# Two-layer graph network on one core: sort ends at groups of 1024 edges, rests of q by TensorE, node update and gated sum rearranged

## The chip, the core and the metric

The kernel runs on one core of a Trainium2 chip. A core has TensorE (PE, matmuls into PSUM; its weight loads have a row of their own, PEld), VectorE (DVE), ScalarE (ACT), GpSimd (POOL) and SyncE (SP, which issues DMAs); each runs its own list of instructions and waits on semaphores for the others. 16 DMA engines move data between the off-chip memory and the on-chip one (SBUF). The metric is the device time of one execution in microseconds (us), the median of several.

## The reference, cut to what matters

A graph attention layer over 200,000 edges that come sorted by `dst`, then a second layer: a small attention over 131,072 unsorted edges, whose sums choose 2 of 4 experts per node.

```python
# layer 1 (6250 nodes, 256 channels, 8 heads), x normalised first
q, k, v = x @ Wq + bq, x @ Wk + bk, x @ Wv + bv
logits = einsum('ehd,ehd->eh', q[dst], k[src]) / sqrt(32)
attn = segment_softmax(logits, dst)
agg = segment_sum(attn * v[src], dst)
h = gelu(agg + x @ Wskip + bskip);  y = x + h;  x2 = layernorm(y) * gamma + beta   (+ the layer's input)
# layer 2, on layernorm(x2)
h = x2n @ W_gat;  a_src, a_dst = sums of h * att_src, h * att_dst
e = leaky_relu(a_src[src] + a_dst[dst]);  alpha = segment_softmax(e, dst)
scores = mean over heads of layernorm(segment_sum(h[src] * alpha, dst) + b_gat)
gates = softmax of the 2 largest of 4 scores, 0 for the others
out = x2 + sum over the 4 experts of gates[e] * (gelu(x2n @ W1[e] + b1[e]) @ W2[e] + b2[e])
```

## The kernel before, in words

Five stages run one after the other, each a block at whose end all engines meet. Nodes are padded to 49 windows (`NW`) of 128 rows, and 7 windows (`CW`) form one of 7 blocks (`NB`).

**prepare** (L201 to L529) does three things at once. (1) For each of 49 windows ("tiles") it normalises x (ACT L542), turns it on TensorE (L474), and makes k and v in one PSUM bank and q and skip in another (L498 the bias, L500 the fp32 products). ACT evacuates both banks (`evacuate`, L562 to L567). q is kept as three bf16 parts whose sum is q: the high part is a cast by ACT (L562), POOL subtracts it (L271), ACT casts that rest into the middle part (L552), and POOL makes the low part with a second subtraction (L275). (2) DVE sorts the 131,072 edges of layer 2 by a bitonic network over a [128, 1024] array of keys `dst << 13 | src`. A step is a minimum and a maximum (L307, L308; L311, L312 where the direction turns). Steps across partitions need the array turned; a `flip` is 8 transposes on TensorE (L514) which DVE (L354) and ACT (L611) copy back, half each. There are 15 flips (`FLIPS`). TensorE does tiles and flips in one fixed order: the table `BETWEEN` says how many tiles stand ahead of each flip, and DVE waits where TensorE comes late. (3) Small tables for the walks over edges, made through `tab_ps`.

**attend** walks over groups of 512 edges of layer 1; POOL gathers their k and v rows. Its loop is the same before and after.

**node_update** (L1097 to L1285) makes x2 and its normalised, transposed form block by block. SP loads `xs` (x, skip and the layer's input, 2688 KB a block, L1107) behind five loads of constants (L1100 to L1104). DVE divides the sums by their denominators, adds skip (L1180), ACT applies gelu, and DVE and ACT normalise twice. At a block's end ACT normalises into `xn2` (L1224), TensorE transposes 14 squares of it (L1278), ACT copies them out (L1231), and TensorE multiplies by `wg` (L1285); each of these waits for the whole of the one ahead.

**route_experts** (L1384 to L1618): POOL gathers one row of a 20-column table per edge of layer 2, 128 edges an instruction, 1024 instructions (L1396). Groups of 8 columns (`RG`, 1024 edges) are summed into windows by one-hot matmuls, a step for each pair of group and window, and the experts' matmuls run between. Ahead of its first gather POOL takes a maximum over the partitions (`partition_all_reduce`, L1386), for which it waits for DVE (L1503).

**route_gates** (L1675 to L1776) makes the gates on DVE, then out = x2 + the four gated expert rows: 28 DVE instructions a block (7 windows, 4 experts, L1776) over four buffers (`SLOTS`); the first buffer is filled at the end of route_experts. SP loads blocks 1 to 3, and then in one list stores block i (L1691), waits for that store to land, and loads block i + 4 (L1683, L1684). It first loads three small rows `rg_con` (L1679).

## Time and profile before

| what | us |
|---|---|
| median of 3 runs | 3990.57 (3986.79 to 3992.12) |
| the profiled execution | 3987.74, of which the span 3985.9 |
| stage prepare | 0 to about 341 |
| attend | about 341 to 2390 |
| node_update | 2390 to 2560 |
| route_experts | 2560 to 3873 |
| route_gates | 3873 to 3986 |

The profile is one execution. A view of stretches gives for each engine its busy time and its instructions in brackets, the TensorE clock granted (1.00 is full speed) and what the DMA engines moved. A timeline gives start, duration, engine, line and operation; the bracket at a row's end is the idle time of the engine ahead of it and what ended it. A row of a line says how often it ran, its busy time and its mean in ns.

### The profile page before, as it was taken

The page shows a single profiled execution, that of the slowest core. Times are in us where ns is not written, and L with a number is a line of the kernel's source. Part 1 is how long each engine was busy: PE and PEld are TensorE (multiplying, and loading weights), DVE is VectorE, ACT ScalarE, POOL GpSimd, SP SyncE. Part 2 cuts the span into 40 slices and gives each one's busy share as a digit, 9 for nine tenths or more (in the row PEclk, how much of TensorE's full clock was granted, in tenths as well). Part 3 has the DMA queues.
Part 4 walks back from the last instruction along what each step waited for, and adds up shares of the span by engine and source line. Part 5 has one row for each costly group of instructions (what it writes and reads, how often), then busy time and mean ns, then how long its engine had stood idle before and what let it go on. Part 6 is the DMA issues. An engine that isn't in the chain of part 4 may idle for free. (4 is left out here: it accounts for less than half of the span.)

```text
span 3985.9 us, 106539 instructions
## 1 busy us (share of the span) xinstructions
PE 3324.8 (83%) x26108; PEld 2449.2 (61%) x26109; DVE 3352.4 (84%) x8812; ACT 2563.2 (64%) x6745; POOL 2589.5 (65%) x2730
## 2 busy tenths in 40 slices
PE   7886999999999999999999992488888888887620
PEld 2334888888788888878888872455555555554410
DVE  8886999999999999999999998667766667666448
ACT  5435888888788888878888875455555555554310
POOL 3225777777677777777777742277777777777750
PEclk9898999999999999999999995599999999999855
DMA  6536888888888888888888857211111111111148
GB/s 218 191 130 200 255 260 256 259 256 261 242 257 255 262 257 257 253 246 257 257 258 258 259 175 246 70 23 33 32 33 32 29 33 33 33 28 33 23 94 309
DMA packets 367692, 683.52 MB, mean 171 GB/s; under 512 B 70294, under 2 KB 240482, under 8 KB 367074
## 3 DMA queue, kind: packets, MB, share of 16 engines
q0 software_dynamic: 157888, 427.05, 38.9%
q1 hardware_dynamic: 183106, 223.68, 16.6%
q10 hardware_dynamic: 26080, 25.70, 2.2%
q8 instruction: 247, 4.05, 0.4%
q14 instruction: 371, 3.04, 0.2%
HBM read 588.41 MB, written 87.78 MB: 170 GB/s over the span
## 5 line engine op out<-in xcount | busy, mean ns | idle before, releaser
L746 POOL DMA_INDIRECT KV<-kv_d,src_i x1564 | 1478.9, 946 | 536.0 <-issue 472.9
L1396 POOL DMA_INDIRECT re_src<-src_tab_d,rsrc x1024 | 982.4, 959 | 312.0 <-issue 244.3
L1012 PE MATMUL agg_ps<-msg,oh 128*128 128x264 f32 x3512 | 889.9, 396 | 1.7 <-DVE agg_ps L830 1.7
L1012 PEld LDWEIGHTS agg_ps<-msg,oh 128*128 128x128 f32 x3512 | 631.6, 190 | 87.5 <-ACT oh L921 1.9
L965 PE MATMUL Q<-q,ohT 128*128 128x256 bf16 x5328 | 659.0, 274 | 1.7
L907 ACT ACTIVATE square<-iota_b,off 128x128 bf16<-128x128 bf16 x1784 | 569.3, 392 | 0.3
L847 DVE TENSOR_REDUCE lg<-prod 128x32 f32<-128x1024 f32 x443 | 540.5, 1220 | 15.3
L835 DVE TENSOR_TENSOR msg<-KV,weigh_ps 128x1056 f32<-128x1056 f32 x439 | 542.5, 1236 | 8.0 <-issue 7.8
L843 DVE TENSOR_TENSOR prod<-KV,Q 128x1024 f32<-128x1024 f32 x443 | 532.6, 1202 | 17.6 <-POOLq L737 13.2
L965 PEld LDWEIGHTS Q<-q,ohT 128*128 128x128 bf16 x5328 | 492.1, 98 | 61.0 <-issue 0.5
L1618 PE MATMUL ex_y_ps<-ex_w,ex_hid 128*112 128x256 f32 x1792 | 440.7, 389 | 0.0
L1606 PE MATMUL ex_h<-acc,ex_w 128*128 (+1 forms) x896 | 417.5, 592 | 3.3 <-PEq L1097 3.3
L1535 ACT COPY re_ohT<-re_ohT_ps 128x1024 bf16<-128x1024 bf16 x179 | 181.1, 1012 | 351.8 <-PE re_ohT_ps L1580 351.1
L891 ACT COPY acc<-agg_ps 128x264 f32 x439 | 166.1, 378 | 329.3 <-PE agg_ps L1012 322.8
L1618 PEld LDWEIGHTS ex_y_ps<-ex_w,ex_hid 128*112 128x112 f32 x1792 | 302.3, 179 | 53.7
L910 ACT ACTIVATE oh<-square,one 128x512 bf16<-128x512 bf16 x446 | 322.0, 722 | 14.5
L921 ACT CAST oh<-oh 128x512 f32<-128x512 bf16 x439 | 273.0, 622 | 0.0
L1434 DVE TENSOR_SCALAR re_oh<-iota_b,re_off 128x128 bf16<-128x128 bf16 x1432 | 254.6, 276 | 6.4
L1580 PE MATMUL re_ohT_ps<-ident_b,re_oh 128*128 128x128 bf16 x1432 | 121.2, 233 | 163.3 <-DVE re_oh L1434 158.0
L914 ACT COPY ohT<-ohT_ps 128x512 bf16<-128x512 bf16 x445 | 255.3, 574 | 3.2 <-PE ohT_ps L955 3.2
L1580 PEld LDWEIGHTS re_ohT_ps<-ident_b,re_oh 128*128 128x128 bf16 x1432 | 89.4, 104 | 232.7 <-DVE re_oh L1434 203.7
L1606 PEld LDWEIGHTS ex_h<-acc,ex_w 128*128 128x128 f32 x896 | 163.0, 202 | 97.1 <-issue 96.6
(264 smaller groups left out, 5662.8 us busy)
## 6 DMA issues: line engine op xcount, KB each, us to landing
q<-q_d SPq DMA_DIRECT2D x446, 192.0 KB
y_d<-ex_y ACTq DMA_DIRECT2D x56, 448.0 KB
KV<-kv_d,src_i POOLq DMA_INDIRECT x1564
nu_xs<-xs_d SPq DMA_DIRECT2D x7, 2688.0 KB, 11.6
rg_ye<-y_d SPq DMA_DIRECT2D x5, 3584.0 KB, 15.6
re_src<-src_tab_d,rsrc POOLq DMA_INDIRECT x1024
kv_d<-pr_kv SPq DMA_DIRECT2D x49, 260.0 KB, 2.2
xs_d<-pr_xs SPq DMA_DIRECT2D x49, 256.0 KB, 2.3
```

Of the source, the lines that this page charges most:

```text
L746: pool.indirect_dma_start(out=KV[:, t % (KVR * G), :], out_offset=None, in_=k.kv_d, in_offset=bass.IndirectOffsetOnAxis(ap=k.src_i[:, t:t ...
L835: v.tensor_tensor(m[:, :, :, :], KV[:, tiles(s), D:KVW].rearrange("p t (h e) -> p t h e", e=HW), bc(p_ps.rearrange("p (t h) -> p t h", h=H ...
L843: v.tensor_tensor(prod[:, :, :], KV[:, tiles(s), 0:D], Q[ring(s, 2)][:, :, :], ALU.mult).then_inc(ok["prod"], 1)
L847: v.reduce_sum(lg[s.slot][:, :], prod[:, :, :].rearrange("p t (h d) -> p (t h) d", d=DH), AX.X).then_inc(ok["lg"], 1)
L907: q = act.activation(square[:, t, :], k.iota_b[:, :], ACT.Square, bias=off[s.slot][:, t:t + 1])
L910: act.activation(oh[ring(s, OHR)][:, :, :], square[:, :, :], ACT.Relu, bias=k.one[:, :], scale=-1.0).then_inc(ok["oh"], 1)
L921: act.copy(oh32[ring(s, 2)][:, :, :], oh[ring(s, OHR)][:, :, :]).then_inc(ok["oh32"], 1)
L965: m = pe.matmul(Q[ring(s, 2)][:, t, :], ohT[ring(s, OHR)][:, t, :], q3[s.slot][:, c * D:(c + 1) * D], start=(c == 0), stop=(c == 2))
L1012: m = pe.matmul(agg_ps[:, 0:HEADS * HW], oh32[ring(s, 2)][:, t, :], msg[ring(s, 2)][:, t, :, :].rearrange("p h e -> p (h e)"), start=False ...
L1396: pool.indirect_dma_start(out=gs[:, t % (RING * RG), :], out_offset=None, in_=k.src_tab_d, in_offset=bass.IndirectOffsetOnAxis(ap=k.rsrc[: ...
L1606: m = pe.matmul(h_ps[f % 2][:, 0:UN], k.w1_sb[:, u.at % NE, c, f * P:(f + 1) * P], k.xT[:, bass.ds(u.block, 1), c, half * UN:(half + 1) * ...
L1618: m = pe.matmul(y_ps[w % 2][0:YN, 0:D], hid[u.at % 2][:, f, w * YN:(w + 1) * YN], k.w2_sb[:, u.at % NE, f, :], start=(f == 0), stop=(f == ...
```

## The change

1. **Sort.** Level 17 of the sort ends once each group of 1024 edges holds its own range of keys: the last ten steps and the last two flips are gone (`FLIPS` 13), and the walk's tables take the group's largest dst (a maximum over 8 columns, a transpose, a maximum, a matmul) and not its last one. The edges of a group lie in another order.
2. **q's rests.** TensorE subtracts the high part and then the middle part from q in its PSUM bank, as a product with minus the identity (`less_hi`, `less_mid`), and ACT casts both rests (`middle`, `lowest`). POOL has no tile work left; ACT has no copy `qf`. The skip part is evacuated second and no longer last. `BETWEEN` has new numbers, and three tiles stand behind the last flip.
3. **node_update.** The first load is cut into three columns of 896 KB and goes ahead of the constants; the first division stands ahead of the wait for the constants; the work at a block's end (normalise, transpose, copy, multiply) is in two parts of 4 and 3 windows.
4. **route_experts.** The maximum over partitions is a transpose, a DVE maximum and a matmul; POOL's gathers wait for nothing of it. SP loads the three small rows here.
5. **route_gates.** Of 7 windows DVE sums 6 (`VT`), TensorE the seventh with diagonal matrices of gates, which ACT makes and whose sum ACT copies out. ACT issues the stores on its own queue, SP only waits for them and loads.

On TensorE in prepare, one tile in the middle of its first twenty; `pr_qs_ps` holds q and skip, `pr_xt` the turned x. Before:

```order
L474 MATMUL pr_xt_ps<-ident,pr_xs0 128x128 x2
L498 MATMUL pr_kv_ps1<-pr_b_parts,pr_ones3 128x512
L500 MATMUL pr_kv_ps1<-pr_w,pr_xt1 128x512 x2
L498 MATMUL pr_qs_ps1<-pr_b_parts,pr_ones3 128x512
L500 MATMUL pr_qs_ps1<-pr_w,pr_xt1 128x512 x2
```

After, with the other window's bank named beside it:

```order
L468 MATMUL pr_xt_ps<-ident,pr_xs4 128x128 x2
L481 MATMUL pr_kv_ps1<-pr_b_parts,pr_ones3 128x512
L483 MATMUL pr_kv_ps1<-pr_w,pr_xt1 128x512 x2
L489 MATMUL pr_qs_ps0<-pr_q3_0,minus_b 128x256
L481 MATMUL pr_qs_ps1<-pr_b_parts,pr_ones3 128x512
L483 MATMUL pr_qs_ps1<-pr_w,pr_xt1 128x512 x2
L493 MATMUL pr_qs_ps0<-pr_q3_0,minus_b 128x256
```

Two bf16 products of 256 columns have come into each tile, both for the window ahead: one between the two banks, one behind them.

On DVE, the end of the sort; the last exchange that is in both, and what follows. Before:

```order
L308 TENSOR_TENSOR so_key<-so_key 128x512
L307 TENSOR_TENSOR so_key<-so_key 128x2x256
L308 TENSOR_TENSOR so_key<-so_key 128x2x256
L307 TENSOR_TENSOR so_key<-so_key 128x4x128
L308 TENSOR_TENSOR so_key<-so_key 128x4x128
L354 COPY so_key<-so_flip 128x512
L307 TENSOR_TENSOR so_key<-so_key 128x8x64
L308 TENSOR_TENSOR so_key<-so_key 128x8x64
```

After:

```order
L298 TENSOR_TENSOR so_key<-so_key 128x512
L425 TENSOR_SCALAR so_dst_i<-so_key 128x1024
L427 CAST rdst<-so_dst_i 128x1024
L429 TENSOR_REDUCE so_most<-rdst 128x128
L431 TENSOR_SCALAR rsrc<-so_key 128x1024
L433 TENSOR_REDUCE so_event<-pp_tab 128x1
```

Three steps, a flip, seven steps and a flip have gone, and two maxima have come in.

On SP in route_gates, from the first store on. Before:

```order
L1691 DMA out_dram<-acc 128x7x256
L1683 DMA acc<-y_d 128x7x1024
L1684 DMA acc<-x_d 128x7x256
L1691 DMA out_dram<-rg_o 128x7x256
L1683 DMA rg_ye<-y_d 128x7x1024
L1684 DMA rg_o<-x_d 128x7x256
L1691 DMA out_dram<-rg_o 128x7x256
```

After, from the load of block 4 on:

```order
L1734 DMA acc<-y_d 128x7x1024
L1735 DMA acc<-x_d 128x7x256
L1734 DMA rg_ye<-y_d 128x7x1024
L1735 DMA rg_o<-x_d 128x7x256
L1734 DMA rg_ye<-y_d 128x7x1024
L1735 DMA rg_o<-x_d 128x7x256
```

The stores have left SP's list and stand in ACT's, each behind the copy of its block's seventh window.

The core of the diff:

```diff
-        FLIPS = 15
+        FLIPS = 13
-        BETWEEN = (20, 2, 2, 2, 2, 2, 2, 2, 2, 2, 2, 2, 2, 2, 3)
+        BETWEEN = (20, 2, 2, 2, 2, 2, 2, 2, 2, 3, 2, 3, 2)
...
-                for w in range(NW + 1):
-                    if w < NW:
-                        pool.wait_ge(ok["qf"], w + 1)
...
-                        pool.tensor_tensor(resid[w % 2][:, :], qf[w % 2][:, :], q3[w % PS][:, 0:D], ALU.subtract).then_inc(ok["resid"], 1)
...
-                        pool.tensor_tensor(q3[u % PS][:, 2 * D:3 * D], resid[u % 2][:, :], q3[u % PS][:, D:2 * D], ALU.subtract).then_inc(ok["lo"], 1)
...
+                    if level < 17:
+                        for b in (9, 8, 7):
+                            plain(P << (b - 7))
+                        flip(meanwhile.get(held["flips"], lambda: None))
+                        for b in range(6, -1, -1):
+                            plain(1 << b)
...
+                def less_hi(w):
+                    pe.wait_ge(ok["hi"], w + 1)
+                    pe.wait_ge(ok["skip"], w + 1)
+                    pe.matmul(qs_ps[w % 2][:, 0:D], k.minus_b[:, :], q3[w % PS][:, 0:D], start=False, stop=True, skip_group_check=True).then_inc(ok["less_hi"], 1)
+
+                def less_mid(w):
+                    pe.wait_ge(ok["mid"], w + 1)
+                    pe.matmul(qs_ps[w % 2][:, 0:D], k.minus_b[:, :], q3[w % PS][:, D:2 * D], start=False, stop=True, skip_group_check=True).then_inc(ok["less_mid"], 1)
...
+                    project(kv_ps[p], p, 0)
+                    if w:
+                        less_hi(w - 1)
+                    if w >= 2:
                         pe.wait_ge(ok["skip"], w - 1)
+                        pe.wait_ge(ok["lo"], w - 1)
+                    project(qs_ps[p], p, 2 * D).then_inc(ok["products"], 1)
+                    if w:
+                        less_mid(w - 1)
...
+                for at, sem in ((D, skip_in), (0, landed[0]), (2 * D, landed[0])):
+                    sp.dma_start(xs[0][:, :, at:at + D], k.xs_d[0:CN, at:at + D].rearrange("(w p) f -> p w f", p=P)).then_inc(sem, 16)
                 sp.dma_start(gam[:, :], bc(gamma.unsqueeze(0), [P, D])).then_inc(const, 16)
...
+                quotients(0, 0)
+                v.wait_ge(const, 80)
...
-                pe.wait_ge(xt_ok, i + 1)
...
+                    for w in range(CW):
+                        if w in (0, parts[1][0]):
+                            pe.wait_ge(xt_ok, i * 2 + (1 if w == 0 else 2))
...
-                pool.wait_ge(ok["max_in"], 1)
-                pool.partition_all_reduce(peak[:, 1, :], peak[:, 0, :], P, bass.bass_isa.ReduceOp.max).then_inc(ok["max"], 1)
...
+                for i in range(SLOTS, NB):
+                    sp.wait_ge(stored[i % SLOTS], (i // SLOTS) * 16)
+                    load(i)
...
+                for i in range(NB):
+                    act.wait_ge(summed, i + 1)
+                    act.copy(o[i % SLOTS][:, VT, :], sum_ps[i % 2][:, 0:D]).then_inc(a_ok, 1)
+                    if i + 2 < NB:
+                        factors(i + 2)
+                    store(i)
...
+                    pe.matmul(sum_ps[i % 2][:, 0:D], k.ident[:, :], o[s][:, VT, :], start=True, stop=False)
+                    for e in range(NE):
+                        m = pe.matmul(sum_ps[i % 2][:, 0:D], diag[i % 2][:, e, :], ye[s][:, VT, e, :], start=False, stop=(e == NE - 1))
```

## Rows read from the trace of the kernel before

**Rows 1.** Four stages: length, busy time of PE, PEld, DVE, ACT, POOL, clock, DMA

```profile
0.00:343.00 343.00, 273.46 (x761) 117.28 (x762) 288.45 (x497) 149.66 (x462) 99.69 (x127) 0.93 0.50 172
...
2390.00:2560.30 170.30, 63.94 (x294) 60.37 (x295) 127.36 (x334) 95.92 (x162) 29.17 (x15) 0.54 0.55 184
2560.30:3873.00 1312.70, 1004.12 (x6952) 645.75 (x6952) 848.50 (x3792) 642.84 (x803) 982.95 (x1026) 0.93 0.19 31
3873.00:3985.90 112.90, 0.00 (x0) 0.00 (x0) 96.53 (x227) 4.13 (x5) 0.00 (x0) 0.50 0.86 313
```

**Rows 2.** Timeline of prepare, DVE: end of the sort, and attend's first instruction

```profile
310.47 0.69 DVE L307 TENSOR_TENSOR so_key<-so_key 128x512 f32<-128x512 f32 x1
...
332.04 1.07 DVE L354 COPY so_key<-so_flip 128x512 f32<-128x512 f32 x1 [3.91 <-PE so_flip L514]
333.58 0.69 DVE L438 TENSOR_SCALAR so_dst_i<-so_key 128x1024 int32<-128x1024 int32 x1 [0.47 <-ACT so_key L611]
...
341.11 0.28 DVE L871 MEMSET msg<- 128x264 f32 x1 [0.41 <-PEq L198]
```

**Rows 3.** Groups of prepare: count, busy us, mean ns; then line 308 alone, min/median/max

```profile
L308 DVE TENSOR_TENSOR so_key<-so_key 128x512 f32<-128x512 f32 x136 | 108.1, 795 | 0.0
...
L308 DVE TENSOR_TENSOR so_key<-so_key x136: 677/684/1194, 47.8 to 327.4; 128x512 f32<-128x512 f32 x136
```

**Rows 4.** Timeline of prepare, POOL and DVE over one tile

```profile
301.15 1.11 POOL L275 TENSOR_TENSOR pr_q<-pr_resid,pr_q 128x256 bf16<-128x256 f32 x1
...
301.66 1.15 DVE L308 TENSOR_TENSOR so_key<-so_key 128x512 f32<-128x512 f32 x1
```

**Rows 5.** Timeline of prepare, TensorE: one tile, the first flips, the last tile

```profile
45.50 0.38 PE L474 MATMUL pr_xt_ps<-ident,pr_xs 128*128 128x128 f32 x2
...
48.36 1.98 PE L500 MATMUL pr_qs_ps<-pr_w,pr_xt 128*128 128x512 f32 x4
50.18 0.38 PE L474 MATMUL pr_xt_ps<-ident,pr_xs 128*128 128x128 f32 x2
...
135.15 1.97 PE L514 MATMUL so_flip<-ident,so_key 128*128 128x128 f32 x8 [9.25 <-DVE so_key L308]
...
149.18 1.04 PE L514 MATMUL so_flip<-ident,so_key 128*128 128x128 f32 x8
...
329.58 1.98 PE L500 MATMUL pr_qs_ps<-pr_w,pr_xt 128*128 128x512 f32 x4
```

**Rows 6.** Timeline of attend, TensorE: twelve bf16 products of 256 columns

```profile
364.86 1.47 PE L965 MATMUL Q<-q,ohT 128*128 128x256 bf16 x12
```

**Rows 7.** Timeline of node_update: its first large load, the add that waits for it

```profile
2392.79 1.04 SPq L1107 DMA_DIRECT2D nu_xs<-xs_d  x2
...
2403.53 2.02 DVE L1180 TENSOR_TENSOR nu_out<-nu_out,nu_xs 128x1792 f32<-128x1792 f32 x1 [3.80 <-DMA nu_xs<-xs_d]
```

**Rows 8.** Timeline of node_update: the last block's end

```profile
2543.93 3.55 ACT L1224 ACTIVATE nu_xn<-nu_x,nu_shift,nu_rstd 128x256 f32<-128x256 f32 x7 [0.47 <-DVE nu_shift L1162]
...
2547.53 3.25 PE L1278 MATMUL nu_turn<-ident,nu_xn 128*128 128x128 f32 x14 [3.75 <-ACT nu_xn L1224]
...
2552.71 4.25 PE L1285 MATMUL nu_h<-nu_wg,acc 128*128 128x24 f32 x28 [1.93 <-ACT acc L1231]
```

**Rows 9.** Timeline of route_experts, POOL: the maximum; then line 1396 alone

```profile
2566.37 0.39 POOL L1386 PARTITION_ALL_REDUCE rt_top<-rt_top  x1 [5.94 <-issue]
...
L1396 POOL DMA_INDIRECT re_src<-src_tab_d,rsrc x1024: 940/944/1490, 2566.9 to 3860.2; - x171
```

**Rows 10.** Timeline of route_gates, DVE: waits, the first and the last block's sum

```profile
3881.24 0.97 DVE L1720 TENSOR_TENSOR rg_s<-rg_s,rg_con 128x784 f32<-128x784 f32 x1 [2.78 <-DMA rg_con<-in_L_ffn_ln_beta_dram]
...
3896.12 11.17 DVE L1776 SCALAR_TENSOR_TENSOR acc<-acc,gates 128x256 f32<-128x256 f32 x28
...
3967.57 11.17 DVE L1776 SCALAR_TENSOR_TENSOR rg_o<-rg_ye,gates,rg_o 128x256 f32<-128x256 f32 x28 [4.86 <-DMA rg_o<-x_d]
```

**Rows 11.** Stretches of route_gates, columns as in Rows 1

```profile
3905.00:3910.00 5.00, 0.00 (x0) 0.00 (x0) 5.00 (x14) 0.00 (x0) 0.00 (x0) 0.50 1.03 409
...
3915.00:3920.00 5.00, 0.00 (x0) 0.00 (x0) 5.00 (x14) 0.00 (x0) 0.00 (x0) 0.50 0.35 90
```

**Rows 12.** DMA issues: KB each, us to landing; of route_gates, then of 0 to 40 us

```profile
out_dram<-acc SPq DMA_DIRECT2D x2, 896.0 KB, 11.7
...
so_ends<-in_L_ffn_edge_index_dram SPq DMA_DIRECT2D x1, 1024.0 KB, 14.1
...
pr_b_parts<-pr_b_part ACTq DMA_DIRECT2D x3, 2.0 KB, 5.2
```

More of the change, by code:

```diff
@@ L158, in prepare @@
         xt = [sb(f"pr_xt{i}", [P, 2, P], F32) for i in range(2)]
-        qf = [sb(f"pr_qf{i}", [P, D], F32) for i in range(2)]
-        resid = [sb(f"pr_resid{i}", [P, D], F32) for i in range(2)]
         xt_ps = ps("pr_xt_ps", [P, 2, P], F32)
@@ L195, in order @@
                 flip(f)
-            assert w == NW
+            while w < NW:
+                tile(w)
+                w += 1
         with nc.Block() as block:
@@ L484, in rows, with project @@
                     t.then_inc(ok["turned_rows"], 1)
+                def project(bank, p, at):
+                    pe.matmul(bank[:, :], ones3[:, :], b_parts[:, at:at + 2 * D], start=True, stop=False)
+                    for c in range(2):
+                        m = pe.matmul(bank[:, :], xt[p][:, c, :], w_sb[:, c, at:at + 2 * D], start=False, stop=(c == 1))
+                    return m
+                def less_hi(w):
[5 more added lines that the diff above has]
+                    pe.matmul(qs_ps[w % 2][:, 0:D], k.minus_b[:, :], q3[w % PS][:, D:2 * D], start=False, stop=True, skip_group_check=True).then_inc(ok["less_mid"], 1)
                 def tile(w):
@@ L523, in _ @@
                 order(tile, flip)
+                less_hi(NW - 1)
+                less_mid(NW - 1)
                 pe.wait_ge(ok["table"], table_at["lasts"])
                 pe.wait_ge(ok["sort"], ready[FLIPS][0])
-                pe.matmul(tab_ps[:, 0:RNG], ends[:, :], k.rdst[:, RG - 1:RT:RG], start=True, stop=True).then_inc(ok["tab_products"], 1)
+                pe.transpose(tab_ps[:, 0:P], r_most[:, :], k.ident[:, :]).then_inc(ok["tab_products"], 1)
                 pe.wait_ge(ok["sort"], ready[FLIPS + 1][0])
+                pe.matmul(tab_ps[:, P:P + RNG], ones[:, :], r_most[:, :], start=True, stop=True).then_inc(ok["tab_products"], 1)
+                pe.wait_ge(ok["sort"], ready[FLIPS + 2][0])
                 pe.matmul(tab_ps[:, 0:RNS], ones[:, :], r_passed[:, :], start=True, stop=True).then_inc(ok["tab_products"], 1)
@@ L566, in evacuate @@
                              kv_ps[p][:, D:2 * D].rearrange("p (h d) -> p h d", d=DH)).then_inc(ok["kv"], 1)
-                    act.copy(xs[w % LOOP][:, D:2 * D], qs_ps[p][:, D:2 * D]).then_inc(ok["skip"], 1)
                 def rows(b):
@@ L1190, in turn @@
                     v.wait_ge(s_gelu, i + 1)
+                    if first and s == 0:
+                        v.wait_ge(landed[0], FIRST_ROWS)
                     ch.on(v.tensor_tensor(out[s][:, :, :], out[s][:, :, :], xs[s][:, :, 0:D], ALU.add))
@@ L1240, in turn @@
                     act.wait_ge(back, i * KB + SHIFT)
-                    normalise(0, out[s], x2[s]).then_inc(norm, 1)
+                    normalise(0, out[s], x2[s], 0, CW).then_inc(norm, 1)
                     if not (first and s == 0):
@@ L1247, in turn @@
                     act.wait_ge(back, (i + 1) * KB)
-                    normalise(1, x2[s], xn2).then_inc(xn_ok, 1)
+                    for a, b in parts:
+                        normalise(1, x2[s], xn2, a, b).then_inc(xn_ok, 1)
                 gelu(0, 0)
@@ L1641, in body @@
                         hidden(u.next(), 3)
+                pe.wait_ge(ok["max_in"], 1)
+                pe.transpose(d_ps[0][0:RH, 0:P], peak[:, :], k.ident[:, :]).then_inc(ok["max"], 1)
+                pe.wait_ge(ok["max_in"], 2)
+                pe.matmul(d_ps[1][:, 0:RH], ones[:, :], peak_diag[:, :], start=True, stop=True).then_inc(ok["max"], 1)
                 pe.wait_ge(k.weights, 64)
@@ L1651, in _, with route_gates @@
                 walk(pe, body)
-def route_gates(nc, k, b_gat, ln_gamma, ln_beta, out):
+def route_gates(nc, k, out):
     with ExitStack() as ctx:
@@ L1827, in graph_layers @@
         k.o0 = free[:, CW * NE * D:CW * (NE + 1) * D].rearrange("p (w f) -> p w f", f=D)
+        at = CW * (NE + 1) * D
+        k.diag = [free[:, at + i * NE * P:at + (i + 1) * NE * P].rearrange("p (e n) -> p e n", n=P) for i in range(2)]
         with ExitStack() as route:
@@ L1840, in graph_layers @@
                 route_experts(nc, k)
-            route_gates(nc, k, b_gat, ln_gamma, ln_beta, out)
+            route_gates(nc, k, out)
 _INS = ["x", "src", "dst"] + ["L0_gnn_" + n for n in ("Wq", "bq", "Wk", "bk", "Wv", "bv", "Wskip", "bskip", "gamma", "beta")] \
```

221 lines of the change are left out of this document (124 added, 97 removed).

## Prediction

> **What bounds the kernel now.** I read the stretches by stage first [rows 1]. The change leaves attend's loop alone, so the four stages shown there are what it can move: 341 us of prepare, 170 of node_update, 1313 of route_experts, 113 of route_gates. Each has another limit, and the average of the engines over the span says little.
>
> In **prepare** DVE (288 us of 343) and TensorE (273) are both near full [rows 1]. The timeline shows who waits for whom. TensorE stood 9.25 us ahead of the first flip, until DVE had sorted [rows 5]: DVE's sort is the bound there. At the last flip it is the other way, DVE waits 3.91 us for TensorE, which was making its last tiles [rows 2]. So the sort sets the end, with TensorE close behind. In **node_update** DVE is the busiest (127 of 170), and only the ends leave room: a wait of 3.80 us for the first load [rows 7], and at the last block a chain ACT, TensorE, ACT, TensorE with nothing beside it [rows 8]. In **route_experts** POOL issues 1024 gathers from 2566.9 to 3861.1, 1.264 us each, of which 0.944 are the instruction [rows 9]: it is the pace, and what delays its first gather delays the stage. In **route_gates** DVE sums for 11.17 us a block, seven times, behind about 23 us of gate arithmetic, with two waits, 2.78 and 4.86 us, for DMA [rows 10].
>
> **Part 1, the sort.** Ten steps and two flips go. They lie between the exchange at 310.47 and the one that reads the keys at 333.58 [rows 2]: 23.1 us of DVE's path. A maximum over 8 columns, one over a transpose and a product come in; the nearest rows are of 0.7 to 1.1 us for 1024 columns [rows 2] and less for the small ones, so about 2 us with their hand-overs.
>
> **Part 2, POOL out of the tiles.** An exchange of line 308 takes 0.684 us at the median and up to 1.194, with a mean of 0.795 [rows 3]; the slow ones are those that lie beside a POOL subtraction, as the one of 1.15 us beside 301.15 [rows 4]. Two readers of the same memory seem to hold each other up. 136 x (0.795 - 0.684) is 15 us for this line alone, and its twin, line 307, runs as often: some 30 us of DVE's path go with POOL's work. By parts 1 and 2 the sort could end near 341.1 - 23 - 30 + 2 = 290. It will not, since TensorE is now late.
>
> **Part 3, TensorE's own sum.** One tile takes 50.18 - 45.50 = 4.68 us [rows 5]. Two bf16 products of 256 columns come in; twelve such took 1.47 us, 0.12 each [rows 6]. I take 0.4 a tile: 0.24 from that row and 0.16, an estimate, for the change of number type beside them. The lower end is 0.24, the upper 1.0, if each also waits for an ACT copy. From 45.50 on stand 45 tiles: 45 x 5.08 = 228.6. 13 flips of 0.9 (1.04 less the overlap, [rows 5]) are 11.7. The small transposes and table products that both versions have are about 10. Four earlier tiles add 1.6, and I leave 1.5 for short waits. 45.5 + 228.6 + 11.7 + 10 + 1.6 + 1.5 = 299 for the end of the last tile, against 329.58 + 1.98 = 331.6 now. TensorE hardly stops, so the slow flips after a wait (1.97 us against 1.04 [rows 5]) go as well. Behind the last tile lay 341.1 - 331.6 = 9.5 us. Now come the two rests of that tile (about 2 us of hand-overs PE, ACT, PE, ACT) and the table chain, 5.8 us before and 1.2 longer: 9 us. Prepare ends at 308, **33 us earlier**. The first flip, now at 135.15, hardly moves (133): DVE is there about 13 us sooner and waits. ACT loses one copy and has one more cast; its order changes, but a rest is asked of it while TensorE makes 2.2 us of other products, so I cost it at nothing. If that cover is gone, the upper end of 1.0 a tile holds.
>
> **Part 4, node_update.** The load that DVE waits for was issued at 2392.79 and used at 2403.53 [rows 7]. It is now cut and goes first, 2.3 us earlier, but the constants, for which DVE also waits ahead of the first add, stand behind all three pieces on one queue: the same 10.6 us from 2390.45, then about 1 us for them and 0.6 us of arithmetic. The add starts at 2402.7, 0.8 us sooner. If small loads pass large ones it is up to 5.5. At the last block the transposes (3.25), copies (1.84 for four) and products (4.25) [rows 8] now run as two parts beside one another: from 2547.5 the last products end near 2553.6 and not 2557.0, 3.4 us. In between DVE is full and nothing is taken from it. **4.2 us.** SP's queue has two more DMAs ahead of the second block's load, which is needed 14 us later.
>
> **Part 5, route_experts.** POOL stood idle 5.94 us until DVE had its maximum and then worked 0.39 [rows 9]. Now the first gather can start at 2560.6 and not at 2566.9: **6.3 us**, and the whole row of gathers moves with it. TensorE's first products start some 3 us later, behind the transposed maximum, and the first sums run up to 5 us behind their gathers; eight groups of buffer and 15 to 30% of free time on PE and DVE take that back.
>
> **Part 6, route_gates.** DVE: the wait of 2.78 us for the small rows goes; 4 of 28 instructions a block go, 7 x 4 x 0.399 = 11.2; the wait of 4.86 us may go [rows 10]. That is 18.8. ACT and TensorE do the seventh window beside it, under 6 us a block against 9.6. But then the transfers are next: after 3913.5 (three loads and the first store) stand three blocks of 4.59 MB and three stores of 0.92 MB. At 400 GB/s, near the 409 of [rows 11], that is 41 us, so the last block is in at 3955.8; DVE would be ready at 3950.5. End of the last sum 3965.3, last store 7.2 us as now (3985.9 - 3978.7): 3972.5, **13.4 us**. The dip to 90 GB/s at 3915 [rows 11], where SP waits 11.7 us for a store behind its own loads [rows 12], goes: a transfer of ACT's queue landed in 5.2 us while SP's took 14.1 [rows 12]. If it stays, 8.
>
> The row says 409 GB/s. Against this stands the Trainium skill, "DMA: Bandwidth & Descriptors", section "Where 436 GB/s comes from", which gives about 358 GB/s as the limit between memory and one core's SBUF. By it those 16.5 MB take 46 us and the gain would be 8.6. The trace is above it, so I keep the row.
>
> **Sum.** 33 + 4.2 + 6.3 + 13.4 = 57 us off the profiled execution's 3987.7: 3930.8. That execution lies 2.8 us under the median of the runs (3990.6), so I forecast **3933**.
>
> **Rivals.** (a) *The slow exchanges are not POOL's doing.* For it: some exchanges beside POOL are not slow. Then DVE sets the last flip near 298 and three tiles and 9 us follow: prepare ends at 323, 15 us worse, 3948. (b) *Slower than before.* TensorE waits in every tile: its product behind the k and v bank needs ACT's casts of the high part and skip, and the next q bank needs the low part of the tile before; these are four hand-overs in turn, where ACT has some 3.6 us of work a tile. It gives 3990 only if a tile grows by 0.4 + 1.2 us (57/49), and is slower than before by over 0.2% beyond 1.3. Against it: the k and v products of 2.2 us lie between. (c) *The same, mild:* 1.0 us more a tile in place of 0.4, some 29 us, 3960. (d) *Transfers in route_gates at about 358 GB/s:* 3938. (e) *Everything cheap:* products at 0.24, constants landing early, the last block not waited for: 8 + 4.7 + 5.3 us less, 3915.
>
> **How the numbers follow.** My forecast, 3933 and within about 12 us of it, 62%; (a) 12%; (b) 3%; (c) 6%; (d) 5%; (e) 12%. The range 3912 to 3954 takes in (a), (d), (e) and leaves out (b), (c) and a tail of the main case. A measurement of this kernel can tell about 0.2% from no change. Faster by more than that 96%, within it 1%, slower 3%.
>
> **What would show it.** In the new profile: no exchange of lines 297 and 298 above 0.75 us in prepare, DVE waiting for TensorE at most flips and no longer the reverse, a tile pace near 5.1 us, attend's first DVE instruction near 308; POOL's first gather within 1 us of its stage's start; the last block's products within 10 us of the last ACT normalise; in route_gates 24 sums a block, 9.6 us, and one wait of about 5 us ahead of the last. I am wrong if a tile takes over 5.6 us, if slow exchanges remain, or if route_experts is not shorter by about 6 us.

## Result, and the profile after

The changed kernel takes 3935.88 us (median, 3934.06 to 3938.15) beside 3989.72 of the kernel before: a ratio of 0.9864, 95% interval 0.9849 to 0.9878. The forecast was 3933, its range 3912 to 3954. The sum was right within 3 us; its terms were not, as the profiled execution (3934.1, span 3932.3) shows when it is cut at the same events as before:

| stage | before | forecast gain | after | gain |
|---|---|---|---|---|
| prepare | 341.1 | 33 | 297.5 | 43.6 |
| attend | 2049.3 | 0 | 2051.4 | -2.1 |
| node_update | 169.8 | 4.2 | 169.5 | 0.3 |
| route_experts | 1312.9 | 6.3 | 1309.3 | 3.6 |
| route_gates | 112.7 | 13.4 | 104.6 | 8.1 |

So prepare gave 10.6 us more than forecast and the other three named stages 11.9 less. The stretches of the changed kernel, to be read against [rows 1]:

```profile
0.00:297.53 297.53, 265.68 (x842) 115.70 (x843) 236.97 (x476) 149.57 (x457) 7.16 (x28) 0.99 0.57 199
```

```profile
2349.00:2518.45 169.45, 65.58 (x294) 62.27 (x294) 127.36 (x334) 95.84 (x161) 29.16 (x15) 0.51 0.55 185
2518.45:3827.65 1309.20, 1007.35 (x6955) 647.22 (x6955) 844.79 (x3795) 642.53 (x803) 985.41 (x1025) 0.93 0.20 31
3827.65:3932.30 104.65, 28.20 (x70) 20.56 (x70) 85.62 (x199) 15.04 (x40) 0.00 (x0) 0.57 0.91 339
```

In prepare TensorE is busy 266 of 298 us, DVE has 51 us less work than in [rows 1], and POOL 7 us where it had 100. The timeline of TensorE in prepare: one tile (answers [rows 5]), the wait that is new, and the last tile.

```profile
33.21 0.38 PE L468 MATMUL pr_xt_ps<-ident,pr_xs 128*128 128x128 f32 x2
33.52 0.39 PE L481 MATMUL pr_kv_ps<-pr_b_parts,pr_ones 3*128 3x512 bf16 x1
33.84 1.99 PE L483 MATMUL pr_kv_ps<-pr_w,pr_xt 128*128 128x512 f32 x4
35.66 0.27 PE L489 MATMUL pr_qs_ps<-pr_q,minus_b 128*128 128x256 bf16 x1
35.87 0.39 PE L481 MATMUL pr_qs_ps<-pr_b_parts,pr_ones 3*128 3x512 bf16 x1
36.18 1.98 PE L483 MATMUL pr_qs_ps<-pr_w,pr_xt 128*128 128x512 f32 x4
38.00 0.27 PE L493 MATMUL pr_qs_ps<-pr_q,minus_b 128*128 128x256 bf16 x1
38.11 0.38 PE L468 MATMUL pr_xt_ps<-ident,pr_xs 128*128 128x128 f32 x2
...
52.48 0.28 PE L493 MATMUL pr_qs_ps<-pr_q,minus_b 128*128 128x256 bf16 x1 [4.52 <-ACT pr_q L567]
...
287.90 1.99 PE L483 MATMUL pr_qs_ps<-pr_w,pr_xt 128*128 128x512 f32 x4
```

A tile takes 38.11 - 33.21 = 4.90 us. And DVE in prepare: one exchange line (answers [rows 3]), then the copies behind the flips, and what DVE waited for ahead of them.

```profile
L298 DVE TENSOR_TENSOR so_key<-so_key x126: 680/684/692, 46.3 to 284.7; 128x512 f32<-128x512 f32 x126
```

```profile
L340 DVE COPY so_key<-so_flip x13: 672/690/692, 131.8 to 275.1; 128x512 f32<-128x512 f32 x13
...
  PE so_flip L525: 29.3, 11
```

The longest exchange of this line is 0.692 us (of its twin, line 297, 0.698), where [rows 3] has up to 1.194, and DVE waits at 11 of 13 flips. These two signs that the prediction named are there. Others are not: a tile takes 4.90 us and not about 5.1, attend's first DVE instruction is at 297.5 and not near 308, DVE waits for DMA ahead of three blocks in route_gates and not of one, and route_experts is shorter by 3.6 us and not by about 6, which the prediction had named as a sign of being wrong (the section on the maximum comes back to it).

### The profile page after: what moved, and what is told of

Read it like the earlier page. It is cut to its first block and busy times, and to the rows that moved or that the text cites. A ratio compares the mean times of both kernels' runs of the same rounds, so it can differ in the third digit from the quotient of the medians.

```text
span 3932.3 us, 106711 instructions
## 1 busy us (share of the span) xinstructions
PE 3355.5 (85%) x26264; PEld 2475.4 (63%) x26265; DVE 3287.6 (84%) x8768; ACT 2575.0 (65%) x6779; POOL 2500.4 (64%) x2631
```

## Experiments

Twelve kernels were run, each from the changed kernel by one edit; full_sort_pool and consts_weights have two, best has three. Stage lengths are those of one profiled execution each; the ratio is to runs of the kernel before on the same chip (medians 3987 to 3993), with an interval of about +-0.0016. That is some 6 us either way, so medians of different chips are compared by their ratios, and a difference of a few us is read from the stages.

| kernel | median | ratio | prepare | attend | node | experts | gates |
|---|---|---|---|---|---|---|---|
| before | 3989.7 | 1 | 341.1 | 2049.3 | 169.8 | 1312.9 | 112.7 |
| after | 3935.9 | 0.9864 | 297.5 | 2051.4 | 169.5 | 1309.3 | 104.6 |
| full_sort | 3945.7 | 0.9889 | 315.5 | 2048.2 | 169.3 | 1308.3 | 103.9 |
| full_sort_pool | 3967.0 | 0.9943 | 335.5 | 2049.1 | 169.1 | 1307.1 | 104.3 |
| short_sort_pool | 3952.8 | 0.9908 | 316.2 | 2051.1 | 167.8 | 1310.4 | 104.9 |
| early_scales | 3926.7 | 0.9842 | 293.2 | 2049.2 | 168.9 | 1309.6 | 104.4 |
| consts_first | 3935.2 | 0.9860 | 298.3 | 2048.7 | 168.6 | 1311.5 | 104.3 |
| consts_weights | 3929.4 | 0.9860 | 299.6 | 2051.5 | 162.3 | 1310.4 | 104.6 |
| one_part | 3937.2 | 0.9875 | 299.7 | 2051.1 | 171.5 | 1309.5 | 105.9 |
| pool_max | 3943.5 | 0.9881 | 296.8 | 2051.3 | 169.1 | 1317.4 | 104.2 |
| dve_all7 | 3940.5 | 0.9872 | 297.7 | 2052.1 | 169.5 | 1310.3 | 106.7 |
| x2_early | 3935.4 | 0.9861 | 297.6 | 2052.2 | 168.7 | 1313.4 | 100.9 |
| sp_stores | 3939.1 | 0.9878 | 299.4 | 2053.0 | 166.8 | 1310.9 | 109.3 |
| best | 3921.7 | 0.9840 | 292.8 | 2051.2 | 164.7 | 1310.8 | 99.8 |

The table is also a measure of chance. Attend, which nothing touches, took 2048.2 to 2053.0 us; prepare with the same code took 296.8 to 299.7. A stage difference under 3 us in one execution says nothing unless a row of that stage explains it, and attend's loss of 2.1 us is inside this spread.

### The sort and POOL, in four combinations

full_sort undoes the shortening of the sort alone:

```diff
-        FLIPS = 13
-        BETWEEN = (20, 2, 2, 2, 2, 2, 2, 2, 2, 3, 2, 3, 2)
+        FLIPS = 15
+        BETWEEN = (20, 2, 2, 2, 2, 2, 2, 2, 2, 2, 2, 2, 2, 2, 2)
...
-                    if level < 17:
-                        for b in (9, 8, 7):
+                    for b in (9, 8, 7):
...
+                flip()
```

full_sort_pool and short_sort_pool give POOL two subtractions a tile that nobody waits for, with the long and the short sort:

```diff
+                for w in range(NW):
+                    for n in ("hi", "mid"):
+                        pool.wait_ge(ok[n], w + 1)
+                        pool.wait_ge(ok["b_rest"], 4 + 2 * w + (n == "mid"))
+                        pool.tensor_tensor(dummy_out[:, :], dummy[:, :], dummy_b[:, :], ALU.subtract).then_inc(ok["b_rest"], 1)
```

> The kernel after, with only the sort back at its full length (15 flips, level 17 to its end); the rests of q stay on TensorE and POOL has no tile work. In the kernel after prepare ends at 297.5 us, every exchange of L297 and L298 takes 0.68 to 0.70 us, and DVE waits 29 us in all for TensorE at 11 flips. Theory A (POOL's subtractions were what slowed DVE, and TensorE is now the pace): the full sort costs less than its 23 us, since the waits at the flips take part of it. DVE's path is the one of before, 341.1, less the 38 us by which the exchanges there were over their undisturbed length: prepare ends at 303 to 308, the time is 3942 to 3946. Theory B (the sort's length alone explains the gain, POOL's work had no part in it): the slow exchanges come back, prepare ends near 335, 3973.

> As full_sort, and POOL does two subtractions of 128x256 a tile again, on tiles of its own that nobody reads, one after the high part and one after the middle part of q is there. Nothing waits for them. Theory A: exchanges beside them take up to 1.2 us, the mean of L298 goes back to about 0.79, and prepare ends at 330 to 341, some 30 us after full_sort: 3970 to 3980. Theory B (rival a of the prediction: the slow exchanges are not POOL's doing): exchanges at 0.69 and the time of full_sort, within 0.2%.

> The kernel after (short sort, rests on TensorE) with the same two idle subtractions a tile on POOL. Theory A: DVE's path grows by some 30 us, of which the waits at the flips (29.3 us, of which 13 or so lie ahead of the first flip) take a part; DVE sets the pace again, prepare ends at 312 to 320, 3951 to 3958. So POOL's work and the last ten steps would each cost about the same alone, and more together than one by one, as the first of them is partly hidden behind TensorE. Theory B: 3936, no change.

Measured ends of prepare: 297.5 (short sort, POOL idle), 315.5 (full, idle), 316.2 (short, busy), 335.5 (full, busy). Theory B falls in all three. The medians of full_sort and short_sort_pool are in the ranges of theory A, that of full_sort_pool is 3 us under its range, and prepare ended some 8 us later in full_sort than I had worked out. That full_sort's median fell into its range all the same is luck: prepare is 18 us longer there, but attend and the three stages behind it were 5.1 us shorter in that execution, and by the ratios the whole kernel is 0.25% (10 us) longer. POOL's idle work costs 18.7 us with the short sort and 20.1 with the long one; the ten steps cost 17.9 and 19.3. Groups of DVE in prepare, full_sort_pool (columns as in [rows 3]):

```profile
L308 DVE TENSOR_TENSOR so_key<-so_key 128x512 f32<-128x512 f32 x136 | 109.6, 806 | 0.0
L307 DVE TENSOR_TENSOR so_key<-so_key 128x512 f32<-128x512 f32 x136 | 107.5, 791 | 8.0 <-ACT so_key L635 3.5
...
L350 DVE COPY so_key<-so_flip 128x512 f32<-128x512 f32 x15 | 10.4, 690 | 13.9 <-PE so_flip L535 13.8
```

And the same lines of full_sort:

```profile
L297 DVE TENSOR_TENSOR so_key<-so_key 128x512 f32<-128x512 f32 x136 | 94.2, 692 | 8.1 <-ACT so_key L625 3.6
L298 DVE TENSOR_TENSOR so_key<-so_key 128x512 f32<-128x512 f32 x136 | 93.2, 685 | 0.0
...
L340 DVE COPY so_key<-so_flip 128x512 f32<-128x512 f32 x15 | 10.3, 690 | 30.0 <-PE so_flip L525 30.0
```

This closes the account. The plain exchanges grow by 16.4 + 13.3 = 29.7 us, the turned ones (31 times each, L311 520 ns against 458 and L312 579 against 454) by 5.8: 35.5 us, which is 0.36 for each of the 98 subtractions. DVE's waits at the flips shrink from 30.0 to 13.8, so 16.2 of it is taken by waits. That leaves 19.3, and 20.1 were measured. One piece of the timeline of full_sort_pool shows the mechanism:

```profile
199.60 0.69 DVE L308 TENSOR_TENSOR so_key<-so_key 128x512 f32<-128x512 f32 x1
199.63 1.18 POOL L275 TENSOR_TENSOR pr_dummy_out<-pr_dummy,pr_dummy_b 128x256 f32<-128x256 f32 x1 [1.23 <-ACT pr_q L577]
...
200.32 1.04 DVE L307 TENSOR_TENSOR so_key<-so_key 128x512 f32<-128x512 f32 x1
```

DVE, which was first, keeps its 0.69; POOL takes 1.18 us and not 0.68, as the one at 201.81 does; the exchange that follows takes 1.04. It looks as if they took turns by whole instructions. The Trainium skill says so ("SBUF — State Buffer", section "SBUF: two separate sides"): a DVE instruction with two SBUF inputs and a GpSimd one that reads SBUF share a port pair by an exclusive lock, and whichever starts first holds it for its whole instruction. These rows agree.

### Is TensorE the pace?

```diff
-                    if level in (4, 5):
-                        scales(level - 3)
+                    if level in (2, 4):
+                        scales(level // 2)
```

> The kernel after, where DVE makes the scales of x's second and third part at levels 2 and 4 of the sort, not 4 and 5. In the kernel after TensorE stands 4.52 us at 52.5 for a tile whose normalise waits for these scales (made at 51.04, though their root was there at 38). Theory A (TensorE is the pace of prepare from its first tile on): the wait goes and every later event of prepare moves 4 to 4.5 us earlier, prepare ends at 293, the time is 3931 to 3932. Theory B (DVE's sort or the arrival of x sets the end): the wait comes back as another one, prepare ends at 297, 3936.

Prepare ends at 293.2, 4.3 us earlier, theory A. TensorE's wait ahead of 52.48 is gone, and the first flip starts at 126.26 and not at 131.21. The wait had cost more than its 4.52 us: behind it the granted clock was 0.53 and four products took 3.54 us and not 1.98. The median, 3926.7, lies under the 3931 to 3932 of theory A, and the ratio fell from 0.9864 to 0.9842; attend was 2.2 us shorter in this execution, and the rest lies within the two intervals. The edit to DVE's list made DVE do nothing faster; it only let TensorE go on.

### The start of node_update

```diff
-                for at, sem in ((D, skip_in), (0, landed[0]), (2 * D, landed[0])):
-                    sp.dma_start(xs[0][:, :, at:at + D], k.xs_d[0:CN, at:at + D].rearrange("(w p) f -> p w f", p=P)).then_inc(sem, 16)
                 sp.dma_start(gam[:, :], bc(gamma.unsqueeze(0), [P, D])).then_inc(const, 16)
...
+                for at, sem in ((D, skip_in), (0, landed[0]), (2 * D, landed[0])):
+                    sp.dma_start(xs[0][:, :, at:at + D], k.xs_d[0:CN, at:at + D].rearrange("(w p) f -> p w f", p=P)).then_inc(sem, 16)
```

> The kernel after, where node_update's five loads of constants go ahead of the three pieces of the first xs again; the piece with skip still goes first among the three. In the kernel after the stage starts at 2348.93, the constants are there at 2361.87, 12.9 us later, and the first add starts at 2362.40. Theory A (what comes last on SP's queue comes last, and the constants stood behind 2.7 MB): the constants land about 5 us after the stage's start, the first add waits for the 0.9 MB of skip and starts 8 to 9 us after it, and as DVE is full behind it the whole stage is 4 to 5 us shorter: 165 us, 3931. Theory B (the whole first load is what is late, whatever stands first): the add moves by under 1 us and the time by nothing. Theory C: the add is early, but DVE then waits for the two other pieces at the second add or for the second block's load, and half of it is given back: 3933.

Theory C, and nearly all of it was given back. SP's queue and DVE in the timeline of the changed kernel (answers [rows 7]):

```profile
2348.93 1.61 SPq L1117 DMA_DIRECT2D nu_xs<-xs_d  x3
2350.58 3.59 SPq L1118 DMA_DIRECT2D nu_gam<-in_L_gnn_gamma_dram  x1
```

```profile
2361.87 0.29 DVE L1201 TENSOR_TENSOR nu_weighted<-nu_wg,nu_att 128x32 f32<-128x32 f32 x2 [9.65 <-DMA nu_att<-in_L_ffn_att_dst_dram]
...
2362.40 2.02 DVE L1195 TENSOR_TENSOR nu_out<-nu_out,nu_xs 128x1792 f32<-128x1792 f32 x1
```

And DVE in consts_first, then SP's queue there:

```profile
2355.89 2.03 DVE L1195 TENSOR_TENSOR nu_out<-nu_out,nu_xs 128x1792 f32<-128x1792 f32 x1 [2.33 <-DMA nu_xs<-xs_d]
...
2392.68 2.03 DVE L1195 TENSOR_TENSOR nu_out<-nu_out,nu_xs 128x1792 f32<-128x1792 f32 x1 [3.40 <-DMA nu_xs<-xs_d]
```

```profile
2364.30 9.11 SPq L1143 DMA_DIRECT2D ex_b<-in_L_ffn_b_dram  x1
2373.44 5.77 SPq L1144 DMA_DIRECT2D ex_b<-in_L_ffn_b_dram  x1
2379.25 0.43 SPq L1135 DMA_DIRECT2D x_d<-nu_x  x1
2379.73 0.56 SPq L1125 DMA_DIRECT2D nu_xs<-xs_d  x1
```

The first add starts 8.9 us after the stage's start (2347.01) and not 13.5, but SP is busy issuing the experts' weights until 2379.21, so block 2's load goes out at 2379.73, 32.7 us after the stage's start where the changed kernel has 34.1, and DVE waits 3.40 us for it. It was a hidden limit, just behind the visible one. consts_weights spreads these issues:

```diff
+                turn(0, 0, True, False)
                 sp.dma_start(k.w1_sb[:, :, :, :], w1.rearrange("e (c p) n -> p e c n", p=P)).then_inc(k.weights, 16)
+                turn(0, 1, True, False)
                 sp.dma_start(k.w2_sb[:, :, :, :], w2.rearrange("e (f p) n -> p e f n", p=P)).then_inc(k.weights, 16)
...
                 turn(half - 1, 0, False, False)
+                sp.dma_start(k.b1_sb[:, :, :], b1.rearrange("e (f p) -> p e f", p=P), allow_slow_non_contiguous=True).then_inc(k.weights, 16)
+                sp.dma_start(k.b2_sb[:, :, :], bc(b2.unsqueeze(0), [P, NE, D])).then_inc(k.weights, 16)
```

> consts_first, where the four loads of the experts' weights (L1141 to L1144 of the kernel after) no longer stand between the loads of blocks 0 and 1 and the first store, but one behind the first turn of SP's list, one behind the second, and two behind the last load. In consts_first the first add was 4.6 us earlier in its stage, but the stage only 0.9 us shorter: DVE waited 3.40 us for block 2's load, whose issue stood behind 23.8 us of issuing the weights, until 2379.21. Theory A (that issue time is what takes the gain back): the load of block 2 is issued as soon as the first store's block is ready, the wait of 3.40 us goes, node_update takes 164.5 to 165.5 us against 168.6 and 169.5. Theory B (the load itself is too slow for the earlier start): the wait stays and the stage takes 168.6.

Theory A: the wait of 3.40 us is gone and the stage takes 162.3 us. 2.7 us of that are the last products at a risen clock (next section) and not the edit's; in best, with the same edit and without that luck, it takes 164.7. The time as a whole does not show it: the ratio is 0.9860 against 0.9864. At their new places the two loads of `ex_b` were issued in 2.95 and 4.42 us, not 9.11 and 5.77.

### The end of a block

```diff
-                            pe.wait_ge(xt_ok, i * 2 + (1 if w == 0 else 2))
+                            pe.wait_ge(xt_ok, i * 2 + 2)
```

and the same for the transposes' and the copies' waits.

> The kernel after, where at a block's end in node_update TensorE, ACT and TensorE each wait for the whole of the step ahead again (as before), and nothing is done in two parts. In the kernel after the last block takes 11.49 us from the start of the last normalise to the end of the last product, in the kernel before 13.03, and the 28 products took 6.14 us at a granted clock of 0.50 against 4.25 at 0.75. Theory A (the pause between transposes and products has nothing to do with the clock; two parts save 3.4 us as worked out, of which a lower clock took 1.9 back in that execution): the chain takes 14.9 us here, with products of 6.1. Theory B (the clock rises in the products when they come later, as before): 13.0 with products of 4.25, so two parts are worth 1.5.

The last block of the changed kernel, which answers [rows 8]:

```profile
2503.25 3.55 ACT L1250 ACTIVATE nu_xn<-nu_x,nu_shift,nu_rstd 128x256 f32<-128x256 f32 x7 [0.47 <-DVE nu_shift L1171]
...
2505.38 3.25 PE L1305 MATMUL nu_turn<-ident,nu_xn 128*128 128x128 f32 x14 [2.97 <-ACT nu_xn L1250]
...
2508.60 6.14 PE L1313 MATMUL nu_h<-nu_wg,acc 128*128 128x24 f32 x28
```

And of one_part:

```profile
2505.51 3.54 ACT L1250 ACTIVATE nu_xn<-nu_x,nu_shift,nu_rstd 128x256 f32<-128x256 f32 x7 [0.47 <-DVE nu_shift L1171]
...
2509.11 3.25 PE L1305 MATMUL nu_turn<-ident,nu_xn 128*128 128x128 f32 x14 [3.69 <-ACT nu_xn L1250]
...
2514.37 4.41 PE L1313 MATMUL nu_h<-nu_wg,acc 128*128 128x24 f32 x28 [2.02 <-ACT acc L1257]
```

The chain takes 13.27 us in one_part (13.03 before) against 11.49: theory B, two parts are worth 1.5 to 1.8 us and not 3.4, as long as the products take 6.14. In the 12 executions with two parts the last 28 products took 6.14 us nine times and 3.64, 3.42 and 3.27 three times (the chain then takes 8.6 to 9.0); in the two with one part 4.25 and 4.41. The stretches of these products, first of the changed kernel, then of [rows 8]:

```profile
2508.60:2514.80 6.20, 6.14 (x29) 6.01 (x28) 0.03 (x1) 0.86 (x2) 0.00 (x0) 0.50 0.00 0
```

```profile
2552.70:2557.00 4.30, 4.25 (x28) 4.13 (x28) 0.00 (x0) 0.00 (x0) 0.00 (x0) 0.75 0.00 0
```

The granted clock is 0.50 in the first, the lower level of 1.2 GHz, and 0.75 in the second, so it rose within the products; in sp_stores, with 3.27 us, it is 1.00. A later start is not what lifts it: in the block ahead of the last, one_part's products start 4.96 us behind the transposes and take 6.14. What lets it rise in one execution and not in the next, these runs don't show.

### The maximum on POOL

```diff
+                pool.wait_ge(ok["max_in"], 1)
+                pool.partition_all_reduce(peak2[:, :], peak[:, :], P, bass.bass_isa.ReduceOp.max).then_inc(ok["max"], 1)
```

> The kernel after with the maximum over partitions back on POOL ahead of its first gather; TensorE's and DVE's part of it is gone. In the kernel after the first gather starts 0.67 us after the stage's start (6.65 before), but the stage is only 3.6 us shorter, since the 1024 gathers take 1296.1 us from the first to the last's start against 1293.3. Theory A (these 2.8 us differ from execution to execution and have nothing to do with the change): the gathers start 6.0 us later, and the stage is 6 us longer than in the kernel after's own shorter executions, 1313 to 1315 or so, 3940 to 3942. Theory B (the early start costs 2.8 us later on): the row of gathers is back at 1293 us and the time is 3939.

The first gather starts 7.52 us after the stage's start and the stage takes 1317.4, 8.1 more and over the range given: theory A, with a first gather that is later by 6.85 and not 6.0, and a time of 3943.5 over its 3940 to 3942. From the first to the last gather's start it takes 1297.3 us here, and 1293.3 to 1300.2 over all fourteen executions; the 1296.1 of the changed kernel is no effect of its early start. POOL in pool_max:

```profile
2524.18 0.39 POOL L1418 PARTITION_ALL_REDUCE rt_top_all<-rt_top  x1 [6.81 <-issue]
2524.75 1.19 POOL L1428 DMA_INDIRECT re_src<-src_tab_d,rsrc  x1 [0.19 <-issue]
```

And in the changed kernel its first gather, then line 1425 alone (answers [rows 9]):

```profile
2519.12 0.95 POOL L1425 DMA_INDIRECT re_src<-src_tab_d,rsrc  x1 [0.53 <-issue]
```

```profile
L1425 POOL DMA_INDIRECT re_src<-src_tab_d,rsrc x1024: 940/944/1366, 2519.1 to 3815.2; - x171
```

### What bounds route_gates

dve_all7 sets `VT = CW` and takes TensorE's and ACT's part out. x2_early loads x2 of blocks 1 to 3 in route_experts:

```diff
+                for i, (t, sem) in enumerate(zip(k.o_early, k.early_in)):
+                    sp.dma_start(t, k.x2_d[(i + 1) * CN:(i + 2) * CN, :].rearrange("(w p) f -> p w f", p=P)).then_inc(sem, 16)
```

sp_stores moves ACT's stores back into SP's list, each ahead of the wait and the load of its buffer:

```diff
-                for i in range(SLOTS, NB):
+                for i in range(NB):
...
+                    sp.wait_ge(added, (i + 1) * NE * VT)
+                    sp.wait_ge(a_ok, copied(i))
+                    if i + 1 < NB:
+                        sp.dma_start(out[i * CN:(i + 1) * CN, :].rearrange("(w p) f -> p w f", p=P), o[s]).then_inc(stored[s], 16)
```

> The kernel after, where DVE sums all seven windows of a block in route_gates (28 instructions, 11.17 us, not 24 and 9.59); TensorE and ACT do no sums, ACT still issues the stores on its own queue. Theory A (the transfers set the stage's end): the waits of 1.16, 4.04 and 4.78 us take up most of the 7 x 1.6 us, what shows is the last block's own 1.6 us and up to 2 us for later stores and loads: 3937 to 3940. Theory B (DVE's sums set it): 11.2 us more, 3947.

> The kernel after, where the 0.9 MB of x2 of blocks 1, 2 and 3 are loaded at the start of route_experts, where the DMA engines move 31 GB/s, into a piece of memory that node_update no longer needs (its first xs buffer lies there now). route_gates has 2.75 MB less to load, everything else is the same. Theory A (route_gates is bound by its transfers from its first microsecond to its last load; DVE waits 1.16, 4.04 and 4.78 us for the last three blocks): at the 400 GB/s of the stage 6.9 us of transfers go, the last block is in 6 to 7 us earlier, and the time is 3929 to 3930. Theory B (the waits are made by the store that each of the last three loads waits for, not by the bytes): the waits stay and the gain is under 2 us.

> The kernel after, where SP issues route_gates' stores in one list with the loads again (store a block, wait for it to land, load the block four further); DVE still sums six windows and TensorE the seventh. The prediction gave the stores' own queue 5.4 us of route_gates' gain (8 without it, 13.4 with it). Theory A: the stores stand behind 4.6 MB loads on SP's queue again, take 12 to 16 us to land and not 7, each of the last three loads is issued that much later, the DMA engines run dry once or twice for 3 to 5 us, and route_gates takes 109 to 111 us against 104.6. Theory B (the transfers bind it either way, since the same bytes move): 104 to 106.

DVE's sums in the changed kernel (answers [rows 10]):

```profile
3848.23 9.59 DVE L1857 SCALAR_TENSOR_TENSOR acc<-acc,gates 128x256 f32<-128x256 f32 x24 [0.17 <-DVE gates L1800]
3857.74 28.58 DVE L1857 SCALAR_TENSOR_TENSOR rg_o<-rg_ye,gates,rg_o 128x256 f32<-128x256 f32 x72
3887.48 9.59 DVE L1857 SCALAR_TENSOR_TENSOR acc<-acc,gates 128x256 f32<-128x256 f32 x24 [1.16 <-DMA acc<-x_d]
3901.11 9.59 DVE L1857 SCALAR_TENSOR_TENSOR rg_o<-rg_ye,gates,rg_o 128x256 f32<-128x256 f32 x24 [4.04 <-DMA rg_o<-x_d]
3915.48 9.59 DVE L1857 SCALAR_TENSOR_TENSOR rg_o<-rg_ye,gates,rg_o 128x256 f32<-128x256 f32 x24 [4.78 <-DMA rg_o<-x_d]
```

Two stretches of it, from 40.4 us on and from the stage's start to the last load's landing:

```profile
3868.10:3915.30 47.20, 13.91 (x30) 9.61 (x30) 37.40 (x95) 4.69 (x16) 0.00 (x0) 0.54 1.04 389
3827.65:3915.48 87.83, 23.56 (x60) 17.36 (x60) 76.04 (x175) 14.67 (x39) 0.00 (x0) 0.56 1.04 392
```

The DMA engines are full (share 1.04) for 87.8 us at 392 GB/s. In dve_all7 7 x 1.6 us more work on DVE cost 2.1: theory A, with a median of 3940.5 at the upper edge of its range; of the three waits one of 1.23 us is left. In sp_stores the stage takes 109.3, 4.7 more, theory A at its lower edge: the waits ahead of the last two blocks are 6.99 and 7.62 us. x2_early lies between its two theories: 3.7 us of the 6.9. The first of the three waits went and the second fell from 4.04 to 1.14, but the last stayed at 4.71. A stretch of x2_early shows why:

```profile
3861.00:3871.00 10.00, 4.88 (x22) 3.64 (x20) 10.00 (x27) 1.55 (x5) 0.00 (x0) 1.00 0.73 257
```

The first three blocks are in earlier, and the engines run dry until block 0 is summed and stored and its buffer can be loaded again. Bytes and buffers bind by turns there. The time as a whole did not move (3935.4), as the gathers took 1300.2 us in that execution, the longest of all; whether the early loads cost the gathers something is not settled. In best, where they are loaded at the same place, they took 1297.7.

Against the rate stands the Trainium skill ("DMA: Bandwidth & Descriptors", section "Where 436 GB/s comes from"), with about 358 GB/s as the limit between memory and one core. By it the 34.4 MB of these 87.8 us would have taken 96. The trace is above it.

### The three together

early_scales, consts_weights and x2_early in one kernel:

> The kernel after with early_scales, consts_weights and x2_early together. The stages by themselves: prepare 293.2 (early_scales), node_update 165 (consts_weights, as expected), route_gates 100.9 (x2_early), against 297.5, 169.5 and 104.6. If the three add up, as they lie in three stages, 12.5 us under the kernel after: 3923 where that takes 3936. If they don't, one of the three stages shows which.

3921.66 us (3920.56 to 3926.10), ratio 0.9840, interval 0.9823 to 0.9856. Prepare 292.8, node_update 164.7, route_gates 99.8: the three stages give 4.7, 4.8 and 4.8 us, 14.3 in all, in the profiled execution, whose span is 12.9 under that of the changed kernel. All four runs are shorter than any of the changed kernel, though the two ratios' intervals overlap. Over early_scales alone the ratio shows nothing (0.9840 against 0.9842): what the other two edits add, 4.8 us each, is read from the stages alone.

## Why the prediction was right, and where not

**Parts 1 and 2, sort and POOL: right, each too large.** POOL's work was to blame for the slow exchanges; rival (a) is refuted by full_sort against full_sort_pool. I put 21 us on the sort and 30 on POOL; alone they are worth 17.9 and 18.7. For the sort, the 23.1 us that I read from [rows 2] hold a wait of 3.91 us for TensorE and four exchanges of 1.04 to 1.16 us beside POOL, so the two parts count some time twice; the forecast for prepare went by TensorE and did not use them. For POOL the step that failed is taking DVE's lost busy time for lost path. With POOL busy DVE still waits 13.8 us at the flips, without it 30.0.

**Part 3, TensorE: right mechanism, the term mis-sized.** It is the pace (early_scales), and sort plus POOL could not give their sum. But a tile takes 4.90 us and not 5.08. I took 0.24 from [rows 6] for the two products and added 0.16 for a change of number type that the trace had not shown; the added cost is 0.22. That makes 45 x 0.18 = 8.1 us, and the last tile ended 9.1 us before 299 (289.9). The two are close by luck, since larger terms met beside it. Where the sum has its tile of 45.50, at 45.5 + 1.6, TensorE already was at 43.01, 4.1 us ahead, for it had started 3.1 us sooner than before. The wait at 52.5 and the slow products behind it then took 6.3. Some 3 us more lie in the other terms, and I have not traced them. Behind the last tile lie 7.6 us and not 9: another 1.4. With the 9.1 these are the 10.5 us by which prepare was too slow in the forecast. The first flip came at 131.2, where I had 133, though TensorE stood 4.52 us at 52.5, a wait that I did not see; its smaller form of before, 1.2 and 0.5 us, I had taken for noise and left 1.5 us for all short waits.

**Part 4, node_update: wrong.** Of 4.2 us 0.3 came. At the start I gave the constants 1 us behind the pieces, so 11.6 us after the stage's start, and the add at 12.2. The first of them alone took 3.59 us to issue behind the pieces; they landed at 12.9, and the add came at 13.5, 0.4 us later than before and not 0.8 earlier. At the end, durations of one execution were used as if they were fixed: the 4.25 us of [rows 8] belong to a clock that rose in them, and the same products took 6.14. The chain gained 1.5 of 3.4. Another 0.5 us was lost in the blocks between and 0.4 behind the last product; I have not traced either.

**Part 5, route_experts: the start right, the stage not settled to 3 us.** The first gather came 5.98 us sooner in its stage, forecast 6.3; the stage gained 3.6 in this pair of executions and 8.1 against pool_max, because the row of 1024 gathers differs by up to 7 us from one execution to the next. One profile of before cannot tell 6.3 from 3.6. With a row of so many equal steps I should have given the term a range.

**Part 6, route_gates: right mechanism, the count wrong.** Transfers are the bound, DVE would have been ready at 77.8 us and the last block was in at 87.8, forecast 82.7. I had the rate (400; 389 measured) but counted three stores behind 40.4 us. There are nearly five: 47.2 us x 389 GB/s = 18.4 MB, of which three blocks are 13.8, against my 16.5. The sum also has a slip of 1 us: 3913.5 + 41.3 is 3954.8 and not 3955.8. And the 5.2 and 14.1 us of [rows 12], which I set side by side for the two queues, are of 2 KB and of 1024 KB; what bears the argument is sp_stores, where a store takes 13 to 16 us until the next load goes out behind it. The stores' own queue is worth 4.7 (forecast 5.4). Rival (d) gave 8.6 us for this stage, and 8.1 came; its mechanism, a rate of 358, is not what happened.

So the total was right in part by luck: an excess of 10.6 us met shortfalls of 11.9 and 2.1.

## What to carry to other kernels

When two cuts on one engine are added, work out what its waits for the next engine become: here 35.5 us of disturbance on DVE were 20.1 us of time, since waits shrank or grew by the difference. Ahead of moving a load forward, read what the same queue issues up to the next load that somebody needs; an issue takes time on the queue's engine even if its data are not urgent. And when a stage is bound by transfers, list every transfer between two events by name, stores too, before any rate is applied.
